# FFN block of a fused AdaLN-attention-FFN kernel: half of the left high products ahead of the rank part, the FFN's banks emptied by ScalarE, two adds on GpSimd

## The reference, cut to what matters

```python
x = x + attn(cond(x, cond_weight[ids_a]), Wq, Wk, Wv, Wo, cos, sin)
x = x + ffn(cond2(x, ids_b, W2, lora_A, lora_B), W_base, b_base, W_router, A, B)

def cond2(x, ids, W, A, B):              # W2 x and a rank-32 part chosen by the batch
    return x @ W.T + (x @ A[ids]) @ B.T * 0.5
def ffn(x, W_base, b_base, W_router, A, B):
    base = x @ W_base.T + b_base
    rw, sel = top_k(x @ W_router.T, 2)   # 8 experts, 2 are chosen
    w = softmax(rw) scattered to 8 columns
    h = einsum('td,erd->ter', x, A)      # 8 experts of rank 16
    return base + einsum('ter,te,eor->to', h, w, B) * 2
```

## Time and profile before

| | us |
|---|---|
| median of the runs | 250.18 (250.13 to 250.23) |
| the profiled execution | 250.14 |
| its span in the profile | 248.4 |
| TensorE busy (matmul) | 231.6, 93% |
| VectorE busy | 186.4, 75% |
| ScalarE busy | 116.4, 47% |
| GpSimd busy | 86.7, 35% |
| granted TensorE clock | full in all 40 slices |

### The profile page before, as it was taken

One profiled execution on the slowest core, in us unless ns is written; L12 is line 12 of the kernel. 1 busy time (PEld: TensorE's weight loads), 2 busy tenths in 40 slices (PEclk: granted clock), 3 DMA queues, 4 the chain that ended last, 5 costly groups with the idle time before them and its releaser, 6 DMA issues.

```text
span 248.4 us, 5752 instructions
## 1 busy us (share of the span) xinstructions
PE 231.6 (93%) x2010; PEld 173.7 (70%) x2010; DVE 186.4 (75%) x923; ACT 116.4 (47%) x261; POOL 86.7 (35%) x93
## 2 busy tenths in 40 slices
PE   6799998989899999999999999999999998989894
PEld 6688975765678676767677767777676764656793
DVE  3788367448957996699769975998599958958763
ACT  3687436587274336523661466156611660154110
POOL 7200663459078006900590049103920230002120
PEclk9999999999999999999999999999999999999999
DMA  5999307024002402160116011601100110002011
GB/s 130 332 383 330 152 16 251 1 56 159 15 11 90 156 1 58 50 204 1 53 48 210 4 53 45 211 4 53 45 0 1 55 43 3 0 4 79 17 45 42
DMA packets 20048, 21.17 MB, mean 85 GB/s; under 512 B 6452, under 2 KB 11572, under 8 KB 20020
## 3 DMA queue, kind: packets, MB, share of 16 engines
q1 hardware_dynamic: 20020, 20.81, 25.8%
HBM read 18.71 MB, written 2.10 MB: 84 GB/s over the span
## 4 chain that ended last, share of the span: by engine, by line
PE 72%; DVE 14%; ACT 4%; issue 3%; SPq 3%; DMA 2%; POOL 1%; DVEq 0%
PE bank L985 12%; PE bank L990 11%; PE bank L986 10%; PE bank L1073 5%; PE bank L996 5%; PE bank L1012 4%; DVE thrown L686 3%; PE bank L1087 3%; PE bank L1046 3%; PE bank L1089 3%; PE bank L1088 3%; DVE late L623 2%; DMA cond_raw<-cond_w_t 2%; PE bank L1039 2%; PE bank L1155 2%
## 5 line engine op out<-in xcount | busy, mean ns | idle before, releaser
L686 DVE CUSTOM_DVE_ANT_0 thrown<-bank,causal 128x128 f32<-128x128 f32 x256 | 56.1, 284 | 0.0
L374 POOL TENSOR_TENSOR rope_b<-rope_a,rope_b 128x128 f32<-128x128 f32 (+1 forms) x16 | 16.3, 1017 | 90.4 <-DVE rope_b L738 90.4
L354 POOL TENSOR_TENSOR cond_w_lo<-cond_raw,cond_w_hi 128x512 fp32r<-128x512 f32 x28 | 35.2, 1289 | 22.9 <-ACT cond_w_hi L419 22.9
L419 ACT ACTIVATE max_rows<-bank,own_p 128x128 fp32r<-128x128 f32 x32 | 9.2, 370 | 35.4 <-PE bank L1022 35.4
L985 PE MATMUL bank<-qkv_w_hi,c_t_hi 128*128 128x512 f32 (+1 forms) x64 | 21.3, 351 | 0.5 <-DVE c_t_lo L623 0.5
L686 DVE DVE_READ_ACCUMULATOR2_ANT neg_max<- 128x1 f32 x256 | 20.9, 82 | 0.0
L383 POOL TENSOR_TENSOR x_bias<-x,bias_row 128x512 f32<-128x512 f32 x8 | 10.3, 1281 | 29.6 <-DVE out_sb L850 28.7
L985 PE MATMUL bank<-fused_w_hi,late 128*128 128x324 f32 (+2 forms) x68 | 20.5, 316 | 0.0
L986 PE MATMUL bank<-qkv_w_lo,c_t_hi 128*128 128x512 f32 (+1 forms) x64 | 20.5, 337 | 0.0
L986 PE MATMUL bank<-fused_w_lo,late 128*128 128x324 f32 (+2 forms) x68 | 19.9, 306 | 0.0
L419 ACT ACTIVATE cond_w_hi<-cond_raw 128x512 fp32r<-128x512 f32 x32 | 17.9, 622 | 1.6 <-DMA cond_raw<-cond_w_t 1.6
(11 more groups left out here) (154 smaller groups left out, 623.0 us busy)
## 6 DMA issues: line engine op xcount, KB each, us to landing
cond_raw<-cond_w_t SPq DMA_DIRECT2D x7, 1024.0 KB, 5.5
xt_raw<-x_t SPq DMA_DIRECT2D x8, 256.0 KB, 5.9
x_nat<-x SPq DMA_DIRECT2D x8, 256.0 KB, 2.7
out<-out_sb SPq DMA_DIRECT2D x8, 256.0 KB, 2.0
stage_d<-base_t SPq DMA_DIRECT2D x4, 256.0 KB, 4.3
cond_raw<-cond_w_t SPq DMA_DIRECT2D x4, 256.0 KB, 4.5
stage_b<-w SPq DMA_DIRECT2D x4, 256.0 KB, 5.7
stage_a<-w_q SPq DMA_DIRECT2D x4, 256.0 KB, 5.7
```

The source lines that it names most:

```text
L354: pool.tensor_tensor(cond_w.lo[:, k, :], cond_raw[:, k, :], f32(cond_w.hi[:, k, :]), ALU.subtract).then_inc(cond_lo, 1)
L374: pool.tensor_tensor(qk[:, at:at + w], rope_a[:, at:at + w], rope_b[:, at:at + w], ALU.add).then_inc(qk_ready, 1)
L419: return nc.scalar.activation(out, in_, ACT.Copy, scale=scale)
L686: nc.vector.tensor_tensor_reduce(thrown[:, p % 2, j, e, :], s_ps[j][:, at:at + P], causal[:, :], -1.0, -MASKED, ALU.add, ALU.min, neg_max[ ...
```

## The change

Five things are changed.

1. TensorE (L1309, L1310): two of the four k-steps of the left half's high products (four matmuls) are issued ahead of `project_low(r)`, in all six rounds. The other two follow it, then the low products and the rank matmul.
2. ScalarE: in rounds 2 to 6 (q = 0 to 4) `empty_left(q)` copies the left bank, 128x324, into `stage_b` at the head of the round, and `empty_right(q)` copies the right bank, 128x512, after `split_c(f)` and ahead of `split_condition(g)`; it waits for `ffn_done`.
3. VectorE: for these batches the copy L801 is gone, the router's logits are read from the copy that ScalarE made, and `add_x_base(q)` and `add_out(q)` are gone from the round.
4. GpSimd: these two adds stand at the head of its round, from SBUF: `add_x_base(q)` (128x188), then `split_a(r)` as before, then `add_out(q)` (128x324 and 128x188).
5. TensorE's waits for the two banks are now on `left_copied` and `right_copied`. The batches 5, 6 and 7, whose experts are chosen after the loop, go as before.

```diff
+        left_raw, right_raw = stage_b[:, 2 * D:2 * D + HALF], stage_b[:, 3 * D:4 * D]
+        emptied = lambda q: q < LAST - 2
 GpSimd
+            def add_x_base(q):
+                pool.wait_ge(left_copied, q + 1)
+                pool.wait_ge(x1b_ready, q + 1)
+                pool.tensor_tensor(x1_bias[:, 0:LEFT], left_raw[:, GATES:HALF], x1_bias[:, 0:LEFT], ALU.add
+                                   ).then_inc(x_base_added, 1)
+            def add_out(q):
+                pool.wait_ge(right_copied, q + 1)
+                pool.wait_ge(x_base_added, q + 1)
+                pool.wait_ge(out_free, 16 * (q + 1))
+                pool.tensor_tensor(out_sb[:, LEFT:], right_raw[:, 0:HALF], x1_bias[:, LEFT:], ALU.add)
+                pool.tensor_tensor(out_sb[:, 0:LEFT], right_raw[:, HALF:D], x1_bias[:, 0:LEFT], ALU.add
+                                   ).then_inc(out_ready, 1)
...
+                if batch(q):
+                    add_x_base(q)
                 if batch(r):
                     split_a(r)
+                if batch(q):
+                    add_out(q)
 ScalarE
+            def empty_left(q):
+                act.wait_ge(gates_done, q + 1)
+                if q > 0:
+                    act.wait_ge(hidden_ready, 6 * q)
+                    act.wait_ge(x_base_added, q)
+                copy(left_raw[:, :], left_ps(q)[:, 0:HALF]).then_inc(left_copied, 1)
+            def empty_right(q):
+                act.wait_ge(ffn_done, q + 1)
+                if q > 0:
+                    act.wait_ge(out_ready, q)
+                copy(right_raw[:, :], right_ps(q)[:, :]).then_inc(right_copied, 1)
...
                 if batch(q):
+                    empty_left(q)
                     exp_top(q)
...
                     split_c(f)
+                if batch(q):
+                    empty_right(q)
 VectorE, choose_experts(q)
+                if emptied(q):
+                    gates = left_raw
+                    dve.wait_ge(left_copied, q + 1)
+                    nc.vector.tensor_reduce(neg_top[:, :], gates[:, 0:EXPERTS], AX_X, ALU.max, negate=True
+                                            ).then_inc(gating, 2)
 VectorE, the round
                     choose_experts(q)
-                    add_x_base(q)
...
-                if batch(q):
-                    add_out(q)
 TensorE
-                        pe.wait_ge(x_base_added, r)
+                        pe.wait_ge(left_copied, r)
...
-                    pe.wait_ge(out_ready, r)
+                    pe.wait_ge(right_copied, r)
...
+                    ffn_high(r, 0, left_ps(r), ks=range(KT // 2))
                     project_low(r)
-                    project_ffn(r, 0, left_ps(r)).then_inc(gates_done, 1)
+                    ffn_high(r, 0, left_ps(r), ks=range(KT // 2, KT))
+                    ffn_low(r, 0, left_ps(r)).then_inc(gates_done, 1)
```

More of the change, by code:

```diff
@@ L159, in build_program @@
         low_rest = sb("low_rest", [P, P])
-        gates = sb("gates", [P, GATES])
+        gates_last = sb("gates_last", [P, GATES])
         top = sb("top", [P, 8])
@@ L205, in build_program @@
             sem("ctx_turned"), sem("inverted"), sem("ctx_scaled"), sem("ctx_normed"), sem("ctx_hi"), sem("ctx_lo"))
+        left_copied, right_copied = sem("left_copied"), sem("right_copied")
         attn_done, x1_ready, x1b_ready = sem("attn_done"), sem("x1_ready"), sem("x1b_ready")
@@ L395, in _ @@
             for t in ROUNDS:
-                f, r, g = t + 1, t - 1, t + 2
+                f, r, q, g = t + 1, t - 1, t - 2, t + 2
                 prep = batch(f) and batch(g)
@@ L799, in choose_experts @@
                 n = 6 * q
[L800 to L804, removed]
+                if emptied(q):
[3 more added lines that the diff above has]
+                                            ).then_inc(gating, 2)
+                else:
+                    gates = gates_last
+                    dve.wait_ge(gates_done, q + 1)
+                    nc.vector.tensor_copy(gates[:, :], left_ps(q)[:, 0:GATES]).then_inc(gating, 1)
+                    dve.wait_ge(gating, n + 1)
+                    nc.vector.tensor_reduce(neg_top[:, :], gates[:, 0:EXPERTS], AX_X, ALU.max, negate=True
+                                            ).then_inc(gating, 1)
                 nc.vector.max(top[:, :], gates[:, 0:EXPERTS]).then_inc(gating, 1)
@@ L818, in gate_hidden @@
             def gate_hidden(q):
+                gates = left_raw if emptied(q) else gates_last
                 n = 6 * q
@@ L848, in add_out @@
                 dve.wait_ge(out_free, 16 * (q + 1))
+                dve.wait_ge(out_ready, q)
                 nc.vector.tensor_tensor(out_sb[:, LEFT:], right_ps(q)[:, 0:HALF], x1_bias[:, LEFT:], ALU.add)
@@ L980, in _, with with_high @@
         def _(pe):
-            def with_high(out, lhs, rhs, cols, landed=None):
-                for k in range(KT):
+            def with_high(out, lhs, rhs, cols, landed=None, ks=range(KT)):
+                for k in ks:
                     if landed is not None:
@@ L1157, in project_low, with ffn_high @@
                 mm.then_inc(low_done, 1)
-            def ffn_high(r, n, to, part=slice(0, HALF)):
+            def ffn_high(r, n, to, part=slice(0, HALF), ks=range(KT)):
                 if r == 0:
@@ L1166, in ffn_high @@
                 pe.wait_ge(x1t_hi, r + 1)
-                with_high(to[:, part], x1_t, fused_w, slice(n * HALF + part.start, n * HALF + part.stop))
+                with_high(to[:, part], x1_t, fused_w, slice(n * HALF + part.start, n * HALF + part.stop), ks=ks)
             def ffn_low(r, n, to, part=slice(0, HALF)):
```

## The result

The changed kernel takes 246.01 us in the median of four runs (245.74 to 246.27), against 250.18 us before: the ratio of the two is 0.9831, with a 95% interval of 0.9818 to 0.9843. The forecast was 245.3 us, with a range of 244.5 to 247.2 us. The profiled execution is one of 245.74 us, its span 244.0 us.

What follows compares the result with a forecast made beforehand. TensorE was taken as the bound: what it issues in a round plus its waits. From 250.14 us, less 2.7 us for the reorder and 2.15 us for VectorE's relief, came 245.3 us, range 244.5 to 247.2 us.

Steps and rivals of the forecast that it cites:

- Both gaps: TensorE idle 0.48 us ahead of `project_low`, for `x1_t`'s low half, and 0.39 us behind `project_out`, for GpSimd's rope sum.
- the control: Round 1, without `add_out`: `project_out` to `project_low` takes 6.14 us, against 6.57 us in round 2, so 0.43 us less.
- The reorder: Four left matmuls ahead of `project_low` bring the rank matmul forward 0.45 us a round, 2.7 us in six rounds.
- the tie between the two paths: At the rank matmul, TensorE's matmuls and VectorE's three steps were to be ready at the same instant within 0.01 us.
- VectorE without its two adds: The rope and what follows come 0.64 us earlier; TensorE gains 0.43 us a round, 2.15 us in rounds 2 to 6.
- The lower bound of 0.23 us: Smallest gain a round from relieving VectorE, if only part of the rope wait counts and `x1` is late next.
- The margin of 0.09 us at `score(t, 2)`: VectorE's maxima, seen by TensorE at 109.90, were to be ready before `score(t, 2)` at 109.99; nothing was counted.
- The first rival: VectorE's L811 loses the port twice, to `split_a` as well; `score(t, 2)` waits 0.38 us in five rounds: 247.2 us, chance 0.13.
- The second: Rival: the 0.43 us isn't from `add_out`, or TensorE waits for `ctx_t` or `x1`; 247.5 us, chance 0.08.
- the third: Rival, slower: GpSimd's `add_out`, about 1.5 us, holds VectorE inside `maxima(t, 2)` and `maxima(t, 3)`; 252.8 us, chance 0.03.
- the forecast's own range: 244.6 us with both terms at their better ends, to 246.5 us with reorder 2.2 us and half the second term.
- the forecast of 1.5 us left: ScalarE's copies ahead of `spread_maxima` were to end by 116.4, 1.5 us ahead of need, and cost nothing.

## Why the prediction was right, and by how much it was off

**The mechanism.** Both gaps named as the ones that the change touches closed, and each part alone gave its share. The prediction counted two waits of TensorE; there was a third, 0.14 us for `ctx_lo`, which closed with the rope's and is in the 0.43 us that the control had measured. TensorE remained the bound.

**The reorder: 0.45 us a round was forecast, 0.41 measured** (3.45 to 3.04 us from the start of the L1053 group to `score(f, 0)`). Of "0.53 us at best, and 0.36 us if it arrives late and has to wait", the second was nearer: the tie between the two paths was real, and it fell on the side of the wait. The rank matmul lasts 0.40 us. The runs with one and three k-steps lie on both sides of it. Six rounds: 2.5 us instead of 2.7.

**VectorE without its two adds: 0.43 us a round was forecast, 0.44 measured.** Round 1 as a control held. What the section put down to "its two adds" is `add_out` alone, as the run with the right bank shows; the move of `add_x_base` earns nothing. The lower bound of 0.23 us, if only a part of the idle 0.39 us were on the path, was not needed.

**The margin of 0.09 us at `score(t, 2)`: this is the step that failed.** "I count nothing" should have been 0.06 us in rounds 3 to 6 and 0.12 us in round 2, 0.4 us in all. Two of its sizes were off. GpSimd's `add_x_base` was put right behind `add_bias`, at 104.2 in the old times; it starts 0.15 us after its end (103.68 to 103.83), as it has to see that add's semaphore first, so the cast ends 0.77 us after `add_bias`, not 0.60. And the maxima begin 0.04 us after the cast's end, where the forecast had them 0.04 us before it: 0.81 us after `add_bias` instead of 0.56. `add_bias` itself came 0.08 us earlier than reckoned, so 0.17 us of lateness met a margin of 0.09. The gates' later way over ScalarE is hidden behind `add_bias` and has no part in it. The run with `split_a` first takes this term away and gives 24.65 us instead of 24.72.

**The first rival** (the cast loses the port twice) did not come: the cast ended with L393, and L374 went behind it. The sign that the prediction gave for it, a wait of `score(t, 2)` for `neg_max`, is there all the same, 0.06 to 0.12 us instead of 0.38 and from the cause above, so the sign alone did not tell them apart. The second and the third found nothing either. L725 took 278 to 292 ns in the changed kernel, 277 to 292 before, with GpSimd's output adds beside it:

```profile
L725 DVE CUSTOM_DVE_ANT_0 thrown<-bank,causal x256: 278/287/292, 35.2 to 210.3; 128x128 f32<-128x128 f32 x128
```

**What the prediction left out.** "The part after the loop is shifted as a whole" overlooked the one wait that the change adds there, 0.18 us.

The sum by measured terms: 6 x 0.41 + 5 x 0.44 - 0.4 - 0.2 = 4.1 us. The medians differ by 4.2 us, the spans by 4.4 us; the profiled execution of the changed kernel was 0.2 us earlier at the end of round 1's scores (74.25 against 74.44), which is start-up.

**Two slips of working.** The ends of the forecast's own range don't follow from its terms: 250.14 - 3.2 - 2.15 is 244.8 us, not 244.6, and 250.14 - 2.2 - 1.1 is 246.8 us, not 246.5. And "6.1 us from `project_out`" to `project_low`, "less the half in front", still holds the idle 0.48 us that the same list says is gone; it is 6.29 us, 5.59 without the half in front.

**ScalarE.** Its idle time ahead of `spread_maxima` fell from 3.78 to 1.90 us; the forecast of 1.5 us left was on the safe side.

```profile
111.56 0.60 ACT L442 ACTIVATE stage_b<-bank 128x512 f32<-128x512 f32 x1 [1.32 <-PE bank L1247]
...
116.67 1.14 ACT L442 ACTIVATE max_rows<-bank,own_p 128x128 fp32r<-128x128 f32 x4 [1.90 <-PE bank L1067]
```

In the repetition of the full change single rounds differ by 0.1 us (24.65 to 24.80 us). The wait for `neg_max` goes with it: in rounds 2 to 6 the idle time in front of L1057's load is 0.31, 0.18, 0.28, 0.19 and 0.30 us. Why the late rounds take turns there is open.

## What to carry to other kernels

When an engine is relieved of work, only the part that stands ahead of somebody's wait counts; find a round or a stage without that step and compare the same stretch. Time taken off one path into a join counts only as far as the other path's margin goes: here TensorE arrived 0.4 us sooner and met VectorE's maxima, with and without the other edit, so both paths have to be worked out to the tenth of a microsecond. And an operation moved to an engine with time to spare is still seen by others, through the port it holds and through the waits it adds: give its place in the queue the same care as the busy engine's.

## What the runs showed of the hardware

- Two small VectorE operations on SBUF end 0.02 to 0.03 us after the GpSimd add that runs beside them, however long that is: a 128x2 `TENSOR_SCALAR` lasts 0.73, 0.80 and 1.22 us so, a 128x2 `CAST` 0.24 and 0.56 us. With no GpSimd add beside them, after the loop, the same two last 0.23 and 0.17 us. The Trainium skill, SBUF — State Buffer, section "SBUF: two separate sides", says that the shared port pair is kept for a whole instruction; the runs agree. Not every operation is held: `TENSOR_REDUCE` and `MAX8` on 128x8, ahead of `top_less`, last 0.16 us beside L388, and the 128x128 operation with one input in PSUM (L725) lasts 278 to 292 ns throughout.
- When a GpSimd instruction ended with VectorE waiting and the next GpSimd instruction at hand, VectorE's went through in every case read here (the cast ahead of L374, L713 ahead of L369). The Trainium skill says in the same section only that whoever starts first keeps the pair.
- One more wait for a semaphore that has long been reached cost 0.18 us on VectorE's `add_out`, which stands on a chain. That is not so everywhere: with `split_a` first, GpSimd's `add_x_base` has two such waits and starts 0.04 us before the end of the add ahead of it in the records (104.15 against 104.19). What makes the difference is open.
- The wait that is late should stand last: for `project_low` 0.26 us from the data to the matmul with another wait behind it, 0.14 us without.
- A GpSimd add that waits for the GpSimd add ahead of it starts 0.15 us after its end; without such a wait it starts 0.05 us before that end in the records (104.83 against 104.88).
